# Row tiles for three small broadcasts on the matrix engine: norms, denominators and the row of key shifts

## What is computed

```python
# layer 0: linear attention over the pixels, 4 heads of 32 channels
norm = jnp.maximum(jnp.sqrt(jnp.sum(x * x, axis=1, keepdims=True)), 1e-12)
xn = x / norm * g[None, :, None, None] * C ** 0.5
qkv = jnp.einsum('bchw,oc->bohw', xn, w_qkv)
...
k = jnp.concatenate([mk, k], axis=-1)
v = jnp.concatenate([mv, v], axis=-1)
q = jax.nn.softmax(q, axis=-2) * scale
k = jax.nn.softmax(k, axis=-1)
context = jnp.einsum('bhdn,bhen->bhde', k, v)
out = jnp.einsum('bhde,bhdn->bhen', context, q)
return jnp.einsum('bchw,oc->bohw', out, w_out) + b_out[None, :, None, None]
# layer 1: a 3 x 3 convolution of every fourth channel, a 1 x 1 one of the others, a bias
out = jax.lax.conv_general_dilated(x, w3m, window_strides=(1, 1), padding=((1, 1), (1, 1)), ...)
out = out + jnp.einsum('oi,bihw->bohw', w1m, x)
out = out + b.sum(axis=1)[None, :, None, None]
```

## Time and profile before

| | before |
|---|---|
| median of 3 runs | 2093.57 us (2093.47 to 2094.22) |
| the profiled execution | 2094.91 us, its span 2093.1 us |
| mean granted TensorE clock | 0.986 of full speed |
| PE busy | 1958.1 us, 94% |
| PE weight loads busy | 1044.2 us, 50% |
| DVE busy | 1736.9 us, 83% |
| ACT busy | 1353.9 us, 65% |
| POOL busy | 1363.3 us, 65% |
| HBM | 68.10 MB read, 67.11 MB written |

### The profile page before, as it was taken

How to read it: one execution, slowest core, us unless ns; L and a number is a source line. 1 busy time by engine, 2 the same in 40 slices (tenths; PEclk the granted TensorE clock), 3 DMA queues, 4 the chain that set the end, 5 groups by cost and what they waited for, 6 DMA issues and landing times.

```text
span 2093.1 us, 50607 instructions
## 1 busy us (share of the span) xinstructions
PE 1958.1 (94%) x21199; PEld 1044.2 (50%) x21199; DVE 1736.9 (83%) x3144; ACT 1353.9 (65%) x1476; POOL 1363.3 (65%) x737
## 2 busy tenths in 40 slices
PE   2889999999999999999999999999999999999996
PEld 0445545555544555544555544555544555554552
DVE  5688888888988888988888988888988888888863
ACT  2567666767666666666666666676766676766661
POOL 5566667766667676666676667676666676666662
PEclk9799999999999999999999999999999999999997
DMA  4367767887667878667787667778777778766675
GB/s 104 61 130 150 154 145 154 168 166 152 146 151 155 170 157 165 147 142 154 167 156 164 151 149 147 163 160 172 147 146 151 156 166 167 152 147 148 134 142 125
DMA packets 349427, 312.96 MB, mean 150 GB/s; under 512 B 299152, under 2 KB 299920, under 8 KB 341008
## 3 DMA queue, kind: packets, MB, share of 16 engines
q1 hardware_dynamic: 347712, 308.73, 70.9%
q10 hardware_dynamic: 1168, 0.98, 0.2%
q0 software_dynamic: 320, 0.01, 0.0%
HBM read 68.10 MB, written 67.11 MB: 65 GB/s over the span
## 4 chain that ended last, share of the span: by engine, by line
PE 67%; DVE 21%; ACT 4%; POOL 3%; DMA 2%; issue 1%; SPq 1%; ACTq 0%
PE pair_ps L799 15%; PE pair_ps L781 8%; PE pair_ps L762 7%; DVE km L1111 7%; PE pair_ps L705 5%; PE bank_ps L699 5%; PE pair_ps L790 4%; PE pair_ps L742 4%; POOL exp_kT_lo L447 3%; PE bank_ps L772 3%; PE pair_ps L765 3%; DVE nrm L1098 2%; DVE parts L1098 2%; PE bank_ps L751 2%; DVE u L1108 2%; PE bank_ps L754 2%
## 5 line engine op out<-in xcount | busy, mean ns | idle before, releaser
L799 PE MATMUL pair_ps<-replicas,w_rep 96*32 96x512 f16 x8192 | 488.9, 383 | 8.9 <-DMA replicas<-yg_lo 8.9
L444 POOL TENSOR_TENSOR u_lo<-u,u_hi 128x1024 f16<-128x1024 f32 x128 | 270.0, 2146 | 273.9 <-ACT u_hi L551 273.9
L447 POOL TENSOR_TENSOR exp_kT_lo<-exp_kT,exp_kT_hi 128x1024 f16<-128x1024 f32 x128 | 301.0, 2361 | 179.1 <-ACT exp_kT_hi L560 179.0
L450 POOL TENSOR_TENSOR u_lo<-exp_q,u_hi 128x1024 f16<-128x1024 f32 x128 | 272.5, 2140 | 113.2 <-ACT u_hi L566 113.2
L799 PEld LDWEIGHTS pair_ps<-replicas,w_rep 96*32 96x32 f16 x8192 | 206.1, 96 | 275.4 <-issue 89.4
L1163 DVE SCALAR_TENSOR_TENSOR image<-pair_ps,image 128x512 f32<-128x512 f32 x256 | 172.2, 681 | 121.9 <-PE pair_ps L799 118.2
L440 POOL TENSOR_SCALAR u<-image,st 128x1024 f32<-128x1024 f32 x128 | 187.9, 1479 | 110.4 <-DVE st L1062 110.4
L551 ACT ACTIVATE u_hi<-u 128x1024 f16<-128x1024 f32 x128 | 130.8, 1045 | 177.6 <-DVE u L1108 177.5
L566 ACT ACTIVATE u_hi<-exp_q 128x1024 f16<-128x1024 f32 x128 | 135.3, 1057 | 161.1 <-DVE exp_q L1150 161.0
L557 ACT ACTIVATE exp_kT<-pair_ps,zcol 128x1024 f32<-128x1024 f32 x128 | 141.0, 1101 | 144.4 <-PE pair_ps L742 144.3
L536 ACT ACTIVATE exp_kT<-u,zcol 128x1024 f32<-128x1024 f32 x128 | 146.0, 1143 | 93.7 <-POOL u L440 92.4
(11 more groups left out here) (179 smaller groups left out, 4832.1 us busy)
## 6 DMA issues: line engine op xcount, KB each, us to landing
image<-in_x SPq DMA_DIRECT2D x256, 256.0 KB, 4.8
out<-image SPq DMA_DIRECT2D x512, 128.0 KB, 2.2
replicas<-yg_hi SPq DMA_DIRECT2D x256, 165.0 KB, 3.9
replicas<-yg_hi SPq DMA_DIRECT2D x256, 107.2 KB, 5.1
replicas<-yg_lo SPq DMA_DIRECT2D x128, 165.0 KB, 4.3
replicas<-yg_lo SPq DMA_DIRECT2D x128, 107.2 KB, 3.8
uT_hi<-u_hi SPq DMA_TRANSPOSE x128, 3.4
uT_lo<-u_lo SPq DMA_TRANSPOSE x128, 3.4
```

The lines of the kernel that those rows point to most:

```text
L444: pool.tensor_tensor(px(UL, v), px(U, v), px(UH, v), ALU.subtract).then_inc(ul_ready, 1)
L447: pool.tensor_tensor(KL[:, v % 2], KT[:, v % 2], KH[:, v % 2], ALU.subtract).then_inc(kl_ready, 1)
L450: pool.tensor_tensor(px(EL, v), px(EQ, v), px(EH, v), ALU.subtract).then_inc(el_ready, 1)
L799: mm = pe.matmul(conv_ps[32 * r:32 * r + 32, j % 2], w_rep[0:32 * SLOTS, tap, r], rep[:, j * ROWS + dy:(j + 1) * ROWS + dy, dx:dx + SIDE], ...
```

## The change

In `broadcast` each product reads only the 32 partitions of `spread` and `parts` that hold bank j's rows, and is given that row tile of the array (`tile_position`). A unit's two products have neighbouring row tiles and write two banks. In `keys` the two products with the shifts become one-row products at rows 0 and 32, and both are issued before the 24 products of the unit. For the second row, `kneg_bf` gets the shifts a second time in column 32 (columns between are zero), the turn has 33 columns, and `krow` 33 partitions. The idle tile is smaller by as much as `kneg_bf` is bigger on 128 partitions.

```diff
-        kneg_bf = sb("kneg_bf", [P, 2], BF16)
+        kneg_bf = sb("kneg_bf", [P, 34], BF16)
...
-        krow = sb("krow", [P, 4, P], BF16)
+        krow = sb("krow", [33, 4, P], BF16)
...
-        idle = sb("idle", [P, 10])
+        idle = sb("idle", [P, 4])
...
             def broadcast(ps, v, done):
                 for j in (2 * v, 2 * v + 1):
-                    mm = pe.matmul(ps[:, (j % 2) * BANK:(j % 2 + 1) * BANK], spread[:, j], parts[:],
-                                   start=True, stop=True)
+                    q = slice(32 * (j % 4), 32 * (j % 4) + 32)
+                    mm = pe.matmul(ps[:, (j % 2) * BANK:(j % 2 + 1) * BANK], spread[q, j], parts[q],
+                                   start=True, stop=True, tile_position=(32 * (j % 4), 0))
                 mm.then_inc(done, 1)
...
             def keys(s, v, ps):
 
                 for half in range(2):
+                    q = slice(32 * half, 32 * half + 1)
+                    pe.matmul(ps[:, half * BANK:(half + 1) * BANK], ones_bf[q], krow[q].rearrange("p a b -> p (a b)"),
+                              start=True, stop=False, skip_group_check=True, tile_position=(32 * half, 0))
+                for half in range(2):
                     bank = ps[:, half * BANK:(half + 1) * BANK]
-                    pe.matmul(bank, ones_bf[:], krow[:].rearrange("p a b -> p (a b)"), start=True, stop=False,
-                              skip_group_check=True)
...
             def turn_k_max(ps):
-                pe.transpose(ps[0:1, 0:P // 2].bitcast(BF16), kneg_bf[:, 0:1], ident_bf[:]).then_inc(max_turned, 1)
+                pe.transpose(ps[0:33, 0:P // 2].bitcast(BF16), kneg_bf[:, 0:33], ident_bf[:]).then_inc(max_turned, 1)
...
-                did(dve.tensor_scalar(kneg_bf[:, 0:1], km[:, 5:6], -1.0, None, ALU.mult))
+                did(dve.tensor_scalar(kneg_bf[:, 0:33:32], km[:, 5:6].to_broadcast([P, 2]), -1.0, None, ALU.mult))
...
             def row_k(s, ps):
-                dve.tensor_copy(krow[0:1], ps[0:1, 0:P // 2].bitcast(BF16).unsqueeze(1).to_broadcast([1, 4, P])
+                dve.tensor_copy(krow[:], ps[0:33, 0:P // 2].bitcast(BF16).unsqueeze(1).to_broadcast([33, 4, P])
                                 ).then_inc(k_max, 1)
...
-            for t in (krow, head_mask, quad_mask, red_norm, red_head):
+            for t in (kneg_bf, head_mask, quad_mask, red_norm, red_head):
                 last = dve.memset(t[:], 0.0)
```

## The result

The changed kernel takes 2064.89 us (median of 4 runs, 2062.98 to 2066.53) against 2093.89 before (4 runs, 2093.47 to 2094.27). The ratio is 0.9861, with a 95% interval of 0.9847 to 0.9875: 29.0 us less, where 32.6 were forecast. The profiled execution took 2065.06 us with a span of 2063.2.

A forecast was written before the change was run, and what follows sets the result against it. PE was taken as nearly the bound, DVE partly limiting. Broadcast savings, keys at nothing, summed to 1.07, less hundredths 1.05 us a sample; times 31 is 32.6 us, from 2093.57 to 2061.0. Range 2050 to 2085; likeliest case alone 2053 to 2070.

The forecast's parts named there:

- What bounds the kernel: Whole kernel: PE, busy 94% of the span, is nearly the bound; time saved is lost where PE then waits for others.
- d = 0.20: Broadcast and key-shift pairs: two row tiles run side by side, saving PE 0.20 us a pair, between 0 and 0.22.
- s = 0.10: PE between products of different form: each added change into or out of row tiles costs 0.10 us, perhaps up to 0.17.
- The rival in which two tiles cost more to enter: Keys, third denominators, first norms: dearer form changes, 2090.5 us at s = 0.17, 2107 at 0.20; chances 0.05 and 0.07.
- Keys at nothing: Four keys units: each pair's saving of 0.20 us is cancelled by two changes of form, so they change nothing.
- Second: it follows the 4-row L819 in the same new form ... +0.20: Second denominators' broadcast: no added change of form, with the way out paid before, so it gains 0.20 us a sample.
- It comes earlier by 0.50 only: Residual before the normalisations: DVE, full behind ACT's result, passes on only 0.50 us of PE's 0.80 us lead.
- The stretch to the first k maximum: From last residual to first k maximum: second and fourth norms' broadcasts shorten DVE's waits for PE, 0.57 us a sample.
- One more element in the negation is a few ns: DVE's negation behind the k maxima, writing two elements instead of one: costs a few ns, counted as nothing.
- The total: Whole kernel: 1.05 us a sample over 31 samples, 32.6 us less, giving 2061.0 us.

The follow-up runs named there:

- same_tile: one_write with both products of a broadcast reading the first bank's 32 rows, in one row tile: 2091.67 us, 0.9988 of the kernel before.
- den_before_value: one_write with the second broadcast of denominators ahead of the value products instead of behind the 4-row product: 2057.63 us.
- bcast_only: The kernel before with only the row tiles in `broadcast`, keys as before: 2048.41 us, 0.978 of before.
- one_write: The changed kernel, but DVE writes only column 0 of `kneg_bf` and PE's turn reads it 33 times: 2048.25 us, 0.978 of before.
- keys_only: The kernel before with only the key shifts changed (two elements written, 33 columns turned, row tiles), broadcasts as before: 2095.58 us, 1.0009 of before.
- forms_a: one_write plus three unread two-element DVE scalar products between the k maxima (column read twice, strided write, float32 to float32): 2144.28 us, one run.
- forms_b: one_write plus three unread DVE instructions between the k maxima (one-element product, two-element sum of two tensors, three-element copy): 2147.40 us, one run.

## Why the prediction was right, and where not

- **What bounds the kernel**: PE nearly everywhere, DVE behind it at the k maxima. Right for the kernel before; the 25.16 us from the first context product to the next parts did not change at all, since no changed product lies in them but one keys unit worth nothing.
- **d = 0.20**: 0.21 measured (0.53 in same_tile against 0.32), and same_tile shows that it comes from the second tile alone.
- **s = 0.10**: measured 0.10 at every way in and out, and again as 9.4 us for one more change and pair in den_before_value. The rival in which two tiles cost more to enter had no ground; L819's overlap in the trace before had told it.
- **Keys at nothing**: right, by bcast_only against one_write (2048.41 and 2048.25).
- **"Second: it follows the 4-row L819 in the same new form ... +0.20"**: this step failed. It gave 0.45. I counted L819 as a product of the same form but not as one of another row tile, beside which the pair could run.
- **"It comes earlier by 0.50 only"** (the residual): 0.87. Up to the first cast behind ACT's result DVE gained 0.75 against the first broadcast (from 14.37 at 1043.43 to 13.62 at 1028.62), the 0.50 and the second broadcast's 0.25. Nearly all of the rest, 0.11, lies between L1163 and the residual, whose starts were 0.72 apart before and are 0.61 apart now. The residual of before started 0.04 after the end of PE's last mix, at 1046.49, so DVE was not full there but waited for PE (its waits for the mixes fell from 17.6 to 11.2 us in all):

```profile
1046.11 0.38 PE L781 MATMUL pair_ps<-u_lo,mt_hi 128*128 128x512 f16 x1
```

- **The stretch to the first k maximum**: the fourth norms and the second normalisation gave 0.64 for 0.57.
- **"One more element in the negation is a few ns"**: the error that mattered most. It cost 0.55 us a sample, 17 us in all (one_write). The step looked at the number of elements, not at what POOL is doing at that moment and whether the longer form waits for it. In the kernel with the old broadcasts DVE reached this place 0.05 us ahead of POOL's end, and so the dearer form was all but harmless there (keys_only: 0.8 us in all). The edit and the gain of the other edits made the cost together.
- **The total**: 32.6 us forecast, 29.0 measured, as 46 from the broadcasts (bcast_only against before, 2094.76 less 2048.41 being 46.4) less 17 for the write. The mechanism of the gain was right and its size was 1.4 times mine. That the total still came near was luck, since the undersized gain and the missed price had opposite signs.

## What to carry to other kernels

Products with few contracted rows are worth row tiles when at least two of them lie next to each other, best next to other few-row products: pairs of 512 columns save 0.21 us and each added change of form costs 0.10, so a lone pair between full products gains nothing. And when a small DVE instruction on the critical chain grows from one element to two, look at POOL: from SBUF to SBUF it may then wait until POOL's running operation ends. A part of a change that is worth nothing by itself, such as the keys here, is best left out, since its side costs remain.

## What the runs showed of the hardware

- A DVE instruction from SBUF to SBUF with two or three elements a partition (one of them a sum of two tensors) ended 0.03 us after the end of POOL's running operation in all five such rows of forms_a and forms_b, and lasted up to 1.12 us there. A one-element one took 0.16 in one_write with 0.71 us of POOL's operation left, and was not held.
- A product of 4 rows at row 0 and two of 32 rows at rows 64 and 96 ran beside each other: all three started within 0.01 us and took 0.41 to the next dense product, where the 4-row product alone took 0.42.
- Entering or leaving 1-row, 4-row and 32-row products costs the same 0.10 us as the 32-column form.
